# First attention of a two-layer block: scores by 32-row matmuls of two heads, four score banks shared by two tiles, one exponential a tile, three banks for maxima

## The reference, cut to what matters

```python
B, S1, S2, DCA = (2, 256, 128, 16)
QDIM, KDIM, H = (256, 128, 16)
HD = QDIM // H
SCALE = HD ** (-0.5)
...
def _attn(q, k, v):
    s = jnp.einsum('bhqd,bhkd->bhqk', q, k) * SCALE
    p = jax.nn.softmax(s, axis=-1)
    return jnp.einsum('bhqk,bhkd->bhqd', p, v)
...
q = _ln((x @ Wq + bq).reshape(b, s1, H, HD), qn_w, qn_b)
kv = jnp.concatenate([y_main @ Wk + bk, y_main @ Wv + bv], axis=-1)
kv = kv.reshape(b, s2, H, 2 * HD)
k = _ln(kv[..., :HD], kn_w, kn_b)
v = kv[..., HD:]
qT = q.transpose(0, 2, 1, 3)
ctx = _attn(qT, k.transpose(0, 2, 1, 3), v.transpose(0, 2, 1, 3))
```

## Time and profile before

| | |
|---|---|
| median of three runs | 2315.67 us (2314.57 to 2316.86) |
| profiled execution: span, first to last instruction | 2312.2 us |
| time of the profiled execution around its span | not given by the page |
| TensorE busy | 2096.5 us (91%) |
| VectorE busy | 1718.1 us (74%) |
| ScalarE busy | 1261.7 us (55%) |
| GpSimd busy | 1259.5 us (54%) |
| exponentials of this stage, first and last start | 865.1 and 1281.7 us |
| mean granted clock of TensorE | 0.937 |

### The profile page before, as it was taken

The page is one execution under the profiler, slowest core; times in us unless marked ns, Lnnn a source line. Parts: engine busy times, 40 slices in busy tenths (PEclk is TensorE's granted clock), DMA queues, the critical chain, the costliest instruction groups (busy, mean ns, idle before and its releaser), DMA issues. The chain is left out here.

```text
span 2312.2 us, 46885 instructions
## 1 busy us (share of the span) xinstructions
PE 2096.5 (91%) x16800; PEld 1711.6 (74%) x16800; DVE 1718.1 (74%) x2372; ACT 1261.7 (55%) x2322; POOL 1259.5 (54%) x1031
## 2 busy tenths in 40 slices
PE   6999999999999579999999786778999999999775
PEld 3887888788788357777777634557899999999763
DVE  5788888888888556666665333758899999999576
ACT  2788888888888216555555212573444444444432
POOL 0566666666666124443343032363898988889430
PEclk6999999999999669999999868888999999999888
DMA  3533323324323312333332053384222323221310
GB/s 95 158 142 115 124 117 139 124 95 161 124 96 136 142 58 100 139 140 117 117 117 87 16 206 93 114 204 167 107 85 108 111 92 114 85 106 44 148 41 16
DMA packets 115781, 260.19 MB, mean 113 GB/s; under 512 B 48001, under 2 KB 85282, under 8 KB 106514
## 3 DMA queue, kind: packets, MB, share of 16 engines
q1 hardware_dynamic: 111810, 247.05, 30.6%
q10 hardware_dynamic: 2304, 7.34, 0.8%
q0 software_dynamic: 1536, 3.94, 0.5%
HBM read 153.97 MB, written 108.28 MB: 113 GB/s over the span
## 5 line engine op out<-in xcount | busy, mean ns | idle before, releaser
L383 DVE TENSOR_REDUCE rk<-n_sq 128x1024 f32 (+2 forms) x384 | 465.7, 1213 | 123.2 <-ACT n_sq L331 120.4
L331 ACT ACTIVATE n_sq<-n_slot 128x1024 f32<-128x1024 f32 (+1 forms) x384 | 394.4, 1027 | 134.9 <-PE n_slot L291 125.7
L289 PE MATMUL n_slot<-n_wh,n_yh 128*128 128x512 f32 (+1 forms) x768 | 318.4, 415 | 2.0 <-PEq L482 2.0
L1735 ACT ACTIVATE a_pr<-a_sc 128x448 f32<-128x448 f32 (+1 forms) x384 | 205.4, 544 | 191.9 <-PE a_sc L1666 179.3
L1799 DVE TENSOR_REDUCE a_mpart<-a_pre 112x2 f32<-112x1024 f32 (+1 forms) x192 | 218.8, 1184 | 119.3 <-PE a_pre L1637 119.3
L291 PE MATMUL n_slot<-n_wh,n_yl 128*128 128x512 f32 (+1 forms) x768 | 303.3, 395 | 0.0
L290 PE MATMUL n_slot<-n_wl,n_yh 128*128 128x512 f32 (+1 forms) x768 | 301.7, 393 | 0.0
L1438 POOL TENSOR_TENSOR p_S<-p_S,a_mb 128x896 f32<-128x896 f32 x94 | 255.2, 2752 | 68.2 <-ACT a_mb L1483 68.2
L1438 POOL TENSOR_TENSOR a_S<-a_S,a_mb 128x896 f32<-128x896 f32 (+1 forms) x89 | 240.8, 2742 | 39.5 <-ACT a_mb L1483 39.5
L263 POOL TENSOR_TENSOR n_khat<-n_kb,n_rs 128x240 f32<-128x240 f32 x192 | 114.6, 597 | 234.6 <-DVE n_rs L398 234.6
L1496 ACT ACTIVATE p_S<-p_S 128x896 f32<-128x896 f32 x96 | 91.5, 953 | 161.2 <-POOL p_S L1438 158.0
(11 more groups left out here) (395 smaller groups left out, 4801.6 us busy)
## 6 DMA issues: line engine op xcount, KB each, us to landing
vdram<-n_v SPq DMA_DIRECT2D x16, 1632.0 KB, 5.3
a_v<-vdram SPq DMA_DIRECT2D x16, 1632.0 KB, 6.9
kTdram<-n_kT SPq DMA_DIRECT2D x16, 1484.0 KB, 5.0
a_kT<-kTdram SPq DMA_DIRECT2D x16, 1484.0 KB, 7.1
n_yT<-in_ctxT SPq DMA_DIRECT2D x16, 750.0 KB, 9.1
yhdram<-n_yh SPq DMA_DIRECT2D x16, 750.0 KB, 6.5
yldram<-n_yl SPq DMA_DIRECT2D x16, 750.0 KB, 8.6
a_yh<-yhdram SPq DMA_DIRECT2D x16, 750.0 KB, 4.2
```

Of the source, the lines that this page charges most:

```text
L289: pe.matmul(dst, high, wh[:, cols], start=True, stop=False)
L331: act.activation(sq[0:n, w, :], slot[w][0:n, :], ACT.Square).then_inc(slot_free, 1)
L383: dve.tensor_reduce(g.rk[0:n, b, j, 8 * s:8 * s + 8], sq[0:n, (2 * j + s) % 3, :].rearrange("p (h d) -> p h d", h=8), X, ALU.add)\
L1735: act.activation(pr[0:n, s % 4, unit, :], sc[(2 * s + unit) % 3][0:n, 0:HALF], ACT.Exp).then_inc(p_ready, 1)
```

## The change

The scores of a half tile are twelve matmuls in place of three: each of the three products is done for the four row groups r of 32 partitions, which hold two heads each, with the 112 query columns of these two heads. Row group r writes to score bank r, at a column offset given by the tile's parity and the half; so both tiles of a step lie in the same four banks. One wait stands ahead of an even tile's scores, for the exponentials of all tiles before it, and ScalarE waits ahead of an even tile for the scores of both tiles of the step. One exponential takes a tile, 4 x 224 columns. `pr` is laid out to match, and `prob` finds a head's 56 columns in it. The maxima have three banks, taken in turn by units: each unit is signalled by itself and reduced by one instruction, and a group waits until the first unit of the group before it has been reduced. The groups have other places in the steps. What is left out of the diff below are the same counts in other waits (`UB` for 12, `NK` for `2 * NK`) and the new names of the `pre` banks in `max_rows`, `denominators` and in VectorE's readers of them.

```diff
-    BETWEEN = {6: (6, 7)}
-    BEHIND = {0: (0, 1), 2: (2, 3), 4: (4, 5), 8: (10, 11)}
-    LAST = {6: (8, 9)}
+    BETWEEN = {}
+    BEHIND = {0: (0,), 2: (2,), 4: (4, 5), 6: (7,), 8: (9, 10)}
+    LAST = {0: (1,), 2: (3,), 4: (6,), 6: (8,), 8: (11,)}
     QP, PV = 2 * NQ, 2
+    PAIRS = range(8)
+    UB = 3 * len(PAIRS)
...
-        pr = sb("pr", [P, 4, 2, HALF])
+        pr = sb("pr", [P, 4, 4, 2 * QP])
...
-        pre = [ctx.enter_context(nc.psum_tensor(f"a0_pre{i}", [P, 2, 512], F32)) for i in range(2)]
-        sc = [ctx.enter_context(nc.psum_tensor(f"a0_sc{i}", [P, 512], F32)) for i in range(3)]
+        pre = ctx.enter_context(nc.psum_tensor("a0_pre", [P, 3, 512], F32))
+        sc = ctx.enter_context(nc.psum_tensor("a0_sc", [P, 4, 512], F32))
...
             def maxima(b, i, group):
...
-                if group >= 2:
-                    pe.wait_ge(pre_max, 12 * b + group - 1)
+                if group >= 1:
+                    pe.wait_ge(pre_max, UB * b + 2 * group - 1)
                 if group % 4 == 0:
                     pe.wait_ge(k_high, 3 * b + chunk + 1)
-                for n, pair in enumerate(pairs):
-                    half, r = pair // 4, pair % 4
-                    mm = pe.matmul(pre[group % 2][0:QP, n, 0:hi - lo], QH[i][32 * r:32 * r + 32, half, r * QP:(r + 1) * QP],
-                                   kh[i][32 * r:32 * r + 32, half, lo:hi], start=True, stop=True)
-                mm.then_inc(pre_psum, 1)
+                for n in range(2):
+                    unit = 2 * group + n
+                    half, r = PAIRS[unit % 8] // 4, PAIRS[unit % 8] % 4
+                    two = slice(32 * r, 32 * r + 32)
+                    pe.matmul(pre[0:QP, unit % 3, 0:hi - lo], QH[i][two, half, r * QP:(r + 1) * QP],
+                              kh[i][two, half, lo:hi], start=True, stop=True).then_inc(pre_psum, 1)
...
             def prob(h, j):
-                return pr[:, j % 4, h // 8, (h % 8) * NQ:(h % 8 + 1) * NQ]
+                at = h // 8 * QP + h % 2 * NQ
+                return pr[:, j % 4, h // 2 % 4, at:at + NQ]
 
             def scores(b, i, j):
...
                 high, low = [m[i][:, :, j * P:j * P + n] for m in (kh, kl)]
+                if j % 2 == 0 and later(t):
+                    pe.wait_ge(p_ready, t)
                 for half in range(2):
                     if j == 0:
                         pe.wait_ge(qm_ready, 2 * b + half + 1)
-                    if later(2 * t + half - 2):
-                        pe.wait_ge(p_ready, 2 * t + half - 2)
-                    dst = sc[(2 * j + half) % 3][0:n, 0:HALF]
-                    pe.matmul(dst, high[:, half], QM[i][:, half, :], start=True, stop=False)
-                    pe.matmul(dst, high[:, half], QL[i][:, half, :], start=False, stop=False)
-                    pe.matmul(dst, low[:, half], QM[i][:, half, :], start=False, stop=True).then_inc(s_ready, 1)
+                    at = j % 2 * 2 * QP + half * QP
+                    for k, (keys, queries) in enumerate(((high, QM[i]), (high, QL[i]), (low, QM[i]))):
+                        for r in range(4):
+                            two = slice(32 * r, 32 * r + 32)
+                            mm = pe.matmul(sc[0:n, r, at:at + QP], keys[two, half],
+                                           queries[two, half, r * QP:(r + 1) * QP], start=(k == 0), stop=(k == 2))
+                mm.then_inc(s_ready, 1)
...
             def step(p, i, pair):
                 for s in range(NK):
                     if held(p):
                         n, t = rows(s), NK * p + s
-                        for unit in range(2):
-                            act.wait_ge(s_ready, 2 * t + unit + 1)
-                            if unit == 0 and later(t - 3):
-                                act.wait_ge(p_used, t - 3)
-                            act.activation(pr[0:n, s % 4, unit, :], sc[(2 * s + unit) % 3][0:n, 0:HALF], ACT.Exp).then_inc(p_ready, 1)
+                        act.wait_ge(s_ready, t + 2 - s % 2)
+                        if later(t - 3):
+                            act.wait_ge(p_used, t - 3)
+                        act.activation(pr[0:n, s % 4, :, :], sc[0:n, :, s % 2 * 2 * QP:(s % 2 + 1) * 2 * QP], ACT.Exp).then_inc(p_ready, 1)
...
             def maximum(b, group):
-                chunk, k = group // 4, 2 * (group % 4)
+                chunk = group // 4
                 lo, hi = CHUNKS[chunk]
-                dve.wait_ge(pre_psum, 12 * b + group + 1)
-                dve.tensor_reduce(mpart[:, chunk, k:k + 2], pre[group % 2][0:QP, :, 0:hi - lo], X, ALU.max).then_inc(pre_max, 1)
+                for unit in (2 * group, 2 * group + 1):
+                    k = PAIRS[unit % 8]
+                    dve.wait_ge(pre_psum, UB * b + unit + 1)
+                    dve.tensor_reduce(mpart[:, chunk, k:k + 1], pre[0:QP, unit % 3, 0:hi - lo], X, ALU.max).then_inc(pre_max, 1)
```

More of the change, by code:

```diff
@@ L1622, in maxima @@
             def maxima(b, i, group):
-                chunk, pairs = group // 4, (2 * (group % 4), 2 * (group % 4) + 1)
+                chunk = group // 4
                 lo, hi = CHUNKS[chunk]
@@ L1644, in max_rows @@
                     for r in range(4):
-                        mm = pe.matmul(pre[0][:, half, r * QP:(r + 1) * QP], sel[:, r, :], dm[:, 4 * half + r, :],
+                        mm = pe.matmul(pre[:, half, r * QP:(r + 1) * QP], sel[:, r, :], dm[:, 4 * half + r, :],
                                        start=(r == 0), stop=(r == 3), skip_group_check=True)
@@ L1683, in denominators @@
                 if held(b + 2):
-                    pe.wait_ge(pre_max, 12 * (b + 2) + 12)
-                pe.matmul(pre[1][:, 0, 0:4 * NQ], den1[:, :], osum[:, :], start=True, stop=True).then_inc(den_ready, 1)
+                    pe.wait_ge(pre_max, UB * (b + 2) + UB)
+                pe.matmul(pre[:, 2, 0:4 * NQ], den1[:, :], osum[:, :], start=True, stop=True).then_inc(den_ready, 1)
             pe.wait_ge(sel_set, 1)
@@ L1760, in spread_low @@
                 if half == 0 and later(b - 1):
-                    pool.wait_ge(s_ready, 2 * NK * (b - 1))
+                    pool.wait_ge(s_ready, NK * (b - 1))
                 spread(QL, i, 1, half).then_inc(ql_built, 1)
@@ L1825, in step @@
                         if later(b - 1):
-                            dve.wait_ge(s_ready, 2 * NK * (b - 1))
+                            dve.wait_ge(s_ready, NK * (b - 1))
                         for half in range(2):
                             dve.wait_ge(mrow, 2 * b + half + 1)
-                            dve.tensor_tensor(QM[1 - i][:, half, :], pre[0][:, half, 0:HALF], QH[1 - i][:, half, :], ALU.add)\
+                            dve.tensor_tensor(QM[1 - i][:, half, :], pre[:, half, 0:HALF], QH[1 - i][:, half, :], ALU.add)\
                                 .then_inc(qm_ready, 1)
@@ L1832, in step @@
                         dve.wait_ge(den_ready, p)
-                        dve.reciprocal(rec[:, :], pre[1][:, 0, 0:4 * NQ]).then_inc(rec_ready, 1)
+                        dve.reciprocal(rec[:, :], pre[:, 2, 0:4 * NQ]).then_inc(rec_ready, 1)
             run(dve, step)
```

7 lines of the change are left out of this document (4 added, 3 removed).

## The result

The changed kernel takes 2494.44 us, the median of four runs (2490.20 to 2495.50), against 2316.27 for the kernel before (four runs, 2314.57 to 2319.60): a ratio of 1.0767 [1.0751, 1.0782]. The forecast was 2316, its range ended at 2350. The profiled execution has a span of 2492.1 us, 179.9 more than before.

What follows compares the result with a forecast made beforehand. TensorE was taken to bound the kernel. From a span of 2312.2 us, batches gave -4.0 and the front +4.8, making 2313.0; 3.5 more for the runs' median gave 2316 us, range 2298 to 2350.

Steps and rivals of the forecast that it cites:

- the clock: TensorE's granted clock in the first attention's batches, taken as 1.00 from a mid-stage stretch of the kernel before.
- rival E: First attention: clock falls to 1.2 GHz in TensorE's new pauses, +100 if throughout, 2418 us; chance 0.04.
- signs of being wrong: Quad outside 0.107 to 0.115, gaps of 0.1 between scores and maxima, or a clock under 1.00 in mid-stage.
- the forecast batch: One batch of the first attention, summed over steps 0 to 10: 26.14 us against 26.37 before.
- The quad: Four score matmuls of four row groups run at once on TensorE, taking 0.111 us together.
- C: Scores: a row group's load waits for its own matmul, quad 0.158, +43, 2359 us; chance 0.10.
- F: Scores: row groups don't run at once with accumulation, quad 0.44, +300; chance 0.03.
- B: Scores: shorter 32-row loads, quads at 0.102, the stage gains another 8, 2308 us; chance of faster 0.33.
- D: Drains between scores and maxima on TensorE, 0.55 a batch, +9, 2325 us; chance 0.18.
- The exponential: ScalarE's exponential over 896 columns, one a tile, takes 0.92 us; the next may start after 0.80.
- A turn: Scores of two tiles, both exponentials and a wait under the TensorE-ScalarE lock: 3.37 us.
- The front: Batch 0's maxima, run alone at the low clock ahead of the batches, take 4.8 us longer.

Runs made afterwards that it cites:

- lockfull: Changed kernel with the score matmuls of the kernel before (128 rows, 448 columns), lock and changed maxima kept; scores one bank a half tile: 2447.69 us, one run.
- wide: Changed kernel with each score matmul streaming 224 query columns in place of 112, same loads and lock, scores wrong: 2398.1 us, one run.
- nolock: lockfull without the lock: two banks a tile, each tile waits for the one two before it: 2379.84 us, ratio 1.0297.
- rows64: Changed kernel with scores in two row groups of 64, 224 columns each, two banks a tile, no lock: 2406.25 us, ratio 1.0376.
- order64: rows64 with the groups of maxima spread, one at each of three places in steps 2 to 8: 2298.77 us, ratio 0.9924.
- afterfill: Changed kernel plus matmuls that nobody reads, 46 a batch where TensorE waits and a few in the front: 2416.19 us, ratio 1.0373.
- tuned64: order64 plus seven unread matmuls ahead of the maxima's row sums and some in the front: 2294.24 us, ratio 0.9910.

## Why the prediction was wrong

**The step that failed** is the clock: every term of the sum was taken at 1.00, from the stretch of before in mid-stage, and carried over to a batch in which TensorE does something else. What the runs showed is a stage at 0.541, with batches of 37.55 us in place of 26.14. That is rival E, "the clock falls to 1.2 GHz in TensorE's new pauses", which stood at a chance of 0.04; its reason is only a part, as lockfull keeps 0.94 with pauses as long. The row was read as a property of the stage; it was one of a TensorE that waited 0.4 us a batch and streamed 448 columns behind each score load. The change took both away: it was to save 6.8 us a batch of streaming, and the prediction itself says that these go into waits. A clock under 1.00 in mid-stage is among its own signs of being wrong.

**E was also priced too low:** +100, from the quads alone. The stage lost 170. At half clock everything of TensorE's on the path takes nearly twice as long. Quads: 0.102 more for each of 46 (those of step 0 lie in the spell at 1.00) are 4.7 us a batch. Products: 1.63 in place of 0.92 (1101.68 to 1103.31), in four steps 2.8. Row sums and denominators: 2.75 (1130.55 to 1133.30) in place of 1.49, 1.3. Groups of maxima up to the products in steps 0, 4 and 8: 0.69, 2.20 and 2.06, against 0.41, 1.59 and 1.49 in wide at 1.00, 1.5. That is 10.3 of the 11.4 over the forecast batch; the rest isn't attributed.

**The other steps held.**
- The quad: 0.111 forecast, 0.112 at 1.00 (median of 584 pairs of loads of one row group) and 0.213 at 0.50 (3876 pairs). wide has 0.112 too, with twice the columns. So C, by which load and matmul of a row group add up, and F are out; B's 0.102 was not seen either.
- D, the drain between scores and maxima: out. At the joint the loads follow 0.03 after those of the scores (1105.80, 1105.83). The rule of the Trainium skill ("TensorEngine Tiling (Array Packing)", Key Properties) that only a change of tiling mode drains agrees.
- The exponential: 0.92 forecast, 0.913 measured. A turn and a batch at 1.00: see wide.
- The front: +4.8 forecast. From the first reduction to the row sums it takes 868.71 - 849.46 = 19.25 against 861.73 - 847.10 = 14.63, +4.62.

**What is shown and what is open.** Shown: that the clock made the loss, since the same lock and loads take the forecast time at 1.00, and a kernel with more TensorE work is faster. Shown too: that the columns behind the loads (0.541 to 0.825, wide) and the pauses (0.998 to 0.943 with the lock, nolock against lockfull) both move the clock; rows64 against order64 points the same way, but there the order of TensorE's work changes along with its waits. wide and lockfull are single runs, and kernels whose clock comes and goes differ by up to 53 us from run to run (afterfill); the 96 us of wide are beyond that. Not settled: how columns and pauses weigh against each other, what brings the clock down in a given batch, and what the changed kernel's own 112-column streams would take at 1.00, since it was never there for a whole batch. In afterfill they take 30.21 at 1.00 with some 5.5 us of unread matmuls, so 24.7 at the least.

By the Trainium skill ("TensorE: Matmul & The Clock Gate", Part 1) the half clock is the default state and activity lifts it. The traces agree in that the stage starts at 0.50 in both kernels; that the prediction weighed this page for its loads and not for its clock is the lapse.

## What to carry to other kernels

Before you cost a change that takes work from TensorE, ask what will fill the time: if nothing does, price the whole stage at the lower clock too (here everything of TensorE's on the path took 1.8 to 1.9 times as long), with a chance to match. The busy share of TensorE in the records was no guide to its clock; read the granted clock, and compare what is streamed per load and how often the engine stops. Spread the other work of the engine, such as the maxima here, so that it doesn't wait at them: that turned +3.8% (rows64) into -0.8% (order64).

## What the hardware showed that I had not expected

- TensorE busy 16.00 of 16 us in the records at a granted clock of 0.50 (tuned64), and 23.20 of 26 at 0.51 in the changed kernel, whose whole stage of 587 us has 0.541.
- Four 32-row matmuls of four row groups run fully at once: four loads of 128 columns in 0.112 us, on rows whose previous matmul was issued one group earlier, with 112 columns behind each load or with 224 (wide).
- Weight loads follow TensorE's clock as matmuls do (0.112 and 0.213 us), while ScalarE's exponentials and VectorE's reductions keep their times (0.913 and 0.668, in the changed kernel as in wide).
- Unread matmuls can pay for themselves: 46 a batch, and some in the front, made the changed kernel 78 us faster.
